# Four chunks of a graph layer's front made ahead instead of five, the fourth late chunk with a row buffer of its own

## The reference

```python
h = jnp.maximum(_layernorm(x, axis=-1), 0.0)          # x: (4096, 256)
rowsum = adj.sum(axis=1)                              # adj: (4096, 4096)
d_inv_sqrt = jnp.where(rowsum > 0, rowsum ** (-0.5), 0.0)
normalized_adj = d_inv_sqrt[:, None] * adj * d_inv_sqrt[None, :]
out = (normalized_adj @ h) @ W + b                    # W: (256, 256)
x = x + relu(out)
```

## Time and profile before

| | |
|---|---|
| median of three runs | 395.7 us (395.69 to 397.05) |
| the profiled execution | 396.11 us, its span 394.3 us |
| TensorE matmuls busy | 383.9 us, 97% of the span |
| VectorE busy | 319.9 us, 81% |
| ScalarE busy | 287.7 us, 73% |
| GpSimd busy | 117.2 us, 30% |
| read from HBM, written | 147.33 MB, 4.22 MB |

### The profile page before, as it was taken

How to read it: one execution, slowest core, us unless ns; L and a number is a source line. 1 busy time by engine, 2 the same in 40 slices (tenths; PEclk the granted TensorE clock), 3 DMA queues, 4 the chain that set the end, 5 groups by cost and what they waited for, 6 DMA issues and landing times.

```text
span 394.3 us, 5160 instructions
## 1 busy us (share of the span) xinstructions
PE 383.9 (97%) x1750; PEld 318.4 (81%) x1750; DVE 319.9 (81%) x313; ACT 287.7 (73%) x283; POOL 117.2 (30%) x278
## 2 busy tenths in 40 slices
PE   6997999999999999999999999999999999999995
PEld 5885788888888888888888888888888888878884
DVE  4948958978686999959689995868889497899997
ACT  2789989888787778678977869787886777365531
POOL 2450675352121126213224831323323223000000
PEclk9999999999999999999999999999999999999998
DMA  8999999999999999999999999999999986898457
GB/s 283 423 421 418 420 421 421 419 422 423 412 421 421 418 421 421 416 422 421 418 421 421 421 415 422 416 419 423 421 419 412 408 310 218 318 369 325 135 190 262
DMA packets 24217, 151.87 MB, mean 385 GB/s; under 512 B 3328, under 2 KB 3328, under 8 KB 7552
## 3 DMA queue, kind: packets, MB, share of 16 engines
q1 hardware_dynamic: 24192, 151.55, 95.1%
HBM read 147.33 MB, written 4.22 MB: 384 GB/s over the span
## 4 chain that ended last, share of the span: by engine, by line
PE 83%; DMA 8%; DVE 3%; ACT 3%; issue 1%; SPq 1%; POOL 1%; DVEq 0%; ACTq 0%; POOLq 0%
PE moved L840 20%; PE moved L842 19%; PE moved L841 19%; PE held L840 6%; PE held L842 6%; PE held L841 6%; DMA out<-nat 3%; DMA out<-turned 3%; PE held L791 2%; DMA acc<-in_x 1%; DMA turned<-in_x_t 1%; ACT nat L398 1%; DVE lo L652 1%; PE moved L775 1%; PE moved L809 1%; PE moved L811 1%
## 5 line engine op out<-in xcount | busy, mean ns | idle before, releaser
L411 ACT ACTIVATE hi<-at,s 128x1024 fp32r<-128x1024 f32 x112 | 123.0, 1145 | 47.3 <-issue 32.4
L840 PE MATMUL moved<-hi,G 128*128 128x512 f32 x384 | 149.9, 390 | 2.6 <-DVE lo L652 1.2
L652 DVE SCALAR_TENSOR_TENSOR lo<-at,s,hi 128x1024 fp32r<-128x1024 f32 x112 | 141.0, 1278 | 12.5 <-ACT hi L411 12.5
L841 PE MATMUL moved<-lo,G 128*128 128x512 f32 x384 | 149.5, 389 | 0.0
L842 PE MATMUL moved<-hi,G 128*128 128x512 f32 x384 | 149.4, 389 | 0.0
L671 DVE TENSOR_TENSOR acc<-moved,acc 128x1024 f32<-128x1024 f32 x84 | 102.7, 1223 | 50.3 <-PE moved L842 50.0
L398 ACT ACTIVATE nat<-nat 128x2048 f32<-128x2048 f32 x64 | 122.0, 1908 | 6.0 <-DMA nat<-in_adj 5.9
L840 PEld LDWEIGHTS moved<-hi,G 128*128 128x128 f32 x384 | 72.1, 188 | 19.1 <-issue 2.9
L842 PEld LDWEIGHTS moved<-hi,G 128*128 128x128 f32 x384 | 72.1, 188 | 15.0
L841 PEld LDWEIGHTS moved<-lo,G 128*128 128x128 f32 x384 | 72.1, 188 | 14.9
L549 POOL TENSOR_TENSOR row_sum<-part 128x1 f32<-128x1 f32 x32 | 18.0, 562 | 182.5 <-ACT nat L398 182.5
(11 more groups left out here) (69 smaller groups left out, 246.3 us busy)
## 6 DMA issues: line engine op xcount, KB each, us to landing
nat<-in_adj SPq DMA_DIRECT2D x64, 1024.0 KB, 13.2
at<-in_adj_t SPq DMA_DIRECT2D x64, 1024.0 KB, 11.9
acc<-in_x SPq DMA_DIRECT2D x4, 512.0 KB, 7.6
nat<-d_dram SPq DMA_DIRECT2D x2, 1024.0 KB, 5.9
nat<-in_x_t SPq DMA_DIRECT2D x4, 512.0 KB, 4.1
turned<-in_x_t SPq DMA_DIRECT2D x4, 512.0 KB, 4.8
out<-nat SPq DMA_DIRECT2D x4, 512.0 KB, 4.9
turned<-in_x SPq DMA_DIRECT2D x3, 512.0 KB, 14.6
```

The costliest lines, as they stand in the source:

```text
L411: nc.scalar.activation(hi[g % RING][:, 2 * c:2 * c + 2, :], at[g % LA][:, 2 * c:2 * c + 2, :], ACT.Copy, scale=s[:, j:j + 1]).then_inc(hi_ ...
L652: nc.vector.scalar_tensor_tensor(out=lo[g % RING][:, tiles, :], in0=at[g % LA][:, tiles, :], scalar=s[:, j:j + 1], in1=hi[g % RING][:, til ...
L840: nc.tensor.matmul(into[:, f, :], big, hi[g % RING][:, t, :], start=begins, stop=False)
L841: nc.tensor.matmul(into[:, f, :], big, lo[g % RING][:, t, :], start=False, stop=False)
```

## The change

AHEAD falls from 5 to 4: chunk 4 is no longer made in the front but late, and the late chunks are made in steps 4, 6, 8 and 10 and projected in steps 5, 7, 9 and 11. The rows of a late chunk get a buffer of their own, late_rows; the wait for the turned buffer moves from the load of the rows to the load of x_late. Chunk 3 is the one in the front that is projected by parts. The fourth early half row is summed on VectorE, with a semaphore of its own. x of chunk 1 is issued from ScalarE's queue. From slot 2 on nat_table is one half row less ahead. TensorE's warming transposes are 16 instead of 14, with five more behind the first turned half chunk. In slot 0 the first block of both panels comes before the second block. ScalarE and VectorE work slot 1 before they take the rounding and the rest of chunk 2's product. The diff, without unchanged code:

```diff
-AHEAD = 5
-MADE_IN = {5: 5, 6: 8, 7: 11}
+AHEAD = 4
+MADE_IN = {4: 4, 5: 6, 6: 8, 7: 10}
...
-FIRST_PART = 4
-WARM = 14
+FIRST_PART = 3
+WARM = 16
+FILL = 5
...
-        end = min(EARLY + min(2 * (g + 1), g + 4) + max(0, g - 20) // 8, 2 * NB)
+        end = min(EARLY + min(2 * (g + 1), g + 3) + max(0, g - 20) // 8, 2 * NB)
...
+        late_rows = sb("late_rows", [P, BW * D])
...
         def h(c):
-            flat = acc[:, c, :, :].rearrange("p f r -> p (f r)") if c < AHEAD else turned[c % 2][:, :]
+            flat = acc[:, c, :, :].rearrange("p f r -> p (f r)") if c < AHEAD else late_rows[:, :]
...
+        def wait_summed(eng, m):
+            eng.wait_ge(nat_summed, m + 1 if m < EARLY - 1 else m)
+            if m >= EARLY - 1:
+                eng.wait_ge(last_early_summed, 1)
...
             def load_x(c):
-                if c >= AHEAD:
-                    sp.wait_ge(hW_done, min(c - 1, AHEAD))
-                    at_least(sp, hT_parts_ready, parts_count(c - 2))
+                if c > AHEAD:
+                    sp.wait_ge(mean_ready, 2 * c)
...
             def save_mean(c):
                 sp.dma_start(means_dram[c - AHEAD], minus_mean[:, c * BW:(c + 1) * BW]).then_inc(mean_saved, DMA)
+                sp.wait_ge(hW_done, min(c - 1, AHEAD))
+                at_least(sp, hT_parts_ready, parts_count(c - 2))
                 sp.dma_start(hT(c), x_late[c - AHEAD]).then_inc(x_late_landed, DMA)
...
             def load_nat(m):
-                at_least(sp, nat_summed, m - LN + 1)
+                if m >= LN:
+                    wait_summed(sp, m - LN)
...
-            load_x(1)
             for c in range(2, AHEAD):
                 load_x(c)
                 load_nat(c - 2)
+            load_nat(EARLY - 2)
             load_nat(EARLY - 1)
...
                 if k == LAST and q == 1:
-                    sp.wait_ge(nat_summed, 2 * NB)
+                    wait_summed(sp, 2 * NB - 1)
...
+            act.dma_start(h(1), x[1]).then_inc(x_landed[1], DMA)
             take_first_half()
...
-                if c >= 2:
-                    sum_nat(c)
-            sum_nat(EARLY - 1)
+            sum_nat(EARLY - 2)
             round_slot(0)
+            round_slot(1)
             round_raw(AHEAD - 2)
-            round_slot(1)
             round_raw(AHEAD - 1)
...
             def scale_of(j):
-                pool.wait_ge(nat_summed, 2 * (j + 1))
+                wait_summed(pool, 2 * j + 1)
...
             rstd_of(0)
-            means_of(4)
             scale_of(0)
...
+            def sum_last_early():
+                m = EARLY - 1
+                dve.wait_ge(nat_landed[m % LN], DMA)
+                nc.vector.reduce_sum(part[:, m // 2, m % 2:m % 2 + 1], nat[m % LN][:, :],
+                                     axis=mybir.AxisListType.X).then_inc(last_early_summed, 1)
...
-            take_stats(1, first)
             centre(0, second)
-            take_stats(1, second)
+            take_stats(1)
             centre(1)
...
+            sum_last_early()
             rest_of_raw(AHEAD - 3)
             rest_of_turned(AHEAD - 1)
             for c in range(2):
                 subtract(0, c)
-            rest_of_raw(AHEAD - 2)
             for c in range(2):
                 subtract(1, c)
+            rest_of_raw(AHEAD - 2)
...
             turn(0, range(BW // 2))
+            for _ in range(FILL):
+                nc.tensor.transpose(moved[1][:, 0, 0:P], ident[:, :], ident[:, :])
...
-            for c, n in ((1, 2), (2, 1), (3, 0)):
-                if n:
-                    project(c, range(n))
+            for c, n in ((1, 2), (2, 1)):
+                project(c, range(n))
                 turn(c + 1)
                 project(c, range(n, BW))
-            project_parts(4)
+            project_parts(3)
             for g, (k, q, panels) in enumerate(SLOTS):
+                if g == 0:
+                    for c in range(WIDTHS[k]):
+                        for p, i in enumerate(panels):
+                            multiply(k, p, i, g, p, c)
+                    continue
```

More of the change, by code:

```diff
@@ L250, in build @@
         nat_summed = sem("nat_summed")
+        last_early_summed = sem("last_early_summed")
         s_ready = sem("s_ready")
@@ L812, in project_parts, with multiply @@
                 mm.then_inc(hW_done, 1)
-            def multiply(k, pos, i, g, p):
-                if i < HELD:
+            def multiply(k, pos, i, g, p, only=None):
+                if only is not None and only > 0:
+                    into = pair_of(("panel", k, i))
+                elif i < HELD:
                     into = held[i]
@@ L824, in multiply @@
                 outer = [(c, f) for f in range(FD) for c in range(WIDTHS[k])] if (k, pos) == (LAST, NP - 1) else \
-                    [(c, f) for c in range(WIDTHS[k]) for f in range(FD)]
+                    [(c, f) for c in range(WIDTHS[k]) for f in range(FD) if only in (None, c)]
                 for c, f in outer:
@@ L847, in multiply @@
                         project_parts(PROJECTING[k])
-                if (k, pos) != (LAST, NP - 1):
+                if (k, pos) != (LAST, NP - 1) and only in (None, WIDTHS[k] - 1):
                     mm.then_inc(panel_done, 1)
```

## The result

The changed kernel takes 400.39 us (median of 6 runs, 399.38 to 400.91), the kernel before 396.96 us on the same chip: ratio 1.0093, 95% interval 1.0077 to 1.0109, so 3.7 us slower. The forecast was slower, 398.0 us; the time lies 0.7 us above the upper end of the range. Part of that distance is the base and not the change: the forecast stands on 395.7 us, the median of three executions of the kernel before, and this comparison on 396.96, the median of six. Against 395.7 the ratio gives 399.4 us, inside the range; the loss itself, 3.7 us by the ratio, is still 1.4 us more than the 2.3 that was forecast. All ratios here compare undisturbed executions; only one was left out as slow, of e11 (556.6 us at a mean granted clock of 0.656).

The account below looks back on a forecast made before the run. TensorE's matmuls bound the kernel from slot 2, with VectorE nearly as full and last at the end. Front -2.15, projection +2.8 and tail +1.6 gave +2.3 us on the profiled execution, median 398.0 us against 395.7; range 395.4 to 399.7.

Parts of the forecast that it names:

- what bounds the kernel: Whole kernel: matmuls set the time from slot 2 on; before it, a chain of 13.0 us from s of block 1.
- the projection: Step 5: the fourth late chunk's 24 matmuls come back on a full TensorE, adding 2.8 us.
- what feeds GpSimd: Front: inputs GpSimd needs before s of block 1 come net 0.3 us later, between 0.8 sooner and 0.5 later.
- the second queue: Front: chunk 1's x from ScalarE's queue delays the first half of chunk 0; 1.1 us loss taken, bounds nothing to 1.25.
- the new order: Front: VectorE's centring of chunk 0's second half no longer waits behind chunk 1's landing and statistics; gain 0.8 us.
- Rival (3): Front: TensorE's pause before chunk 3's matmuls drops the clock to 0.50, costing up to 1.5 us: 399.5; chance 0.08.
- the front: Start to slot 2: s of block 1 at 28.3, 2.15 us sooner, so slot 2 at 41.3.
- the tail: From slot 55: G of block 31 one slot later delays x_out and slot 59; +1.6 us, bounds 0 and 2.2.
- nothing gives it back, tail +1.6: Tail: VectorE, 1.6 us late at slot 59, has no idle time behind it, so the kernel ends 1.6 later.
- (1): Tail: x_out lands in time, costing at most 0.7 us; kernel not slower, 396.3 to 397.1; chance 0.20.
- (2): Front: chunk 1 lands beside chunk 0 without harm, s of block 1 at 26.9: 396.5; chance 0.09 alone, 0.08 with (1).
- (4): Front: chain not relieved, ScalarE's third sum or slot 0 itself late; gain only 1 us, 399.1; chance 0.07.

Follow-up runs that it names:

- e11: Kernel before with the changed front edits, five chunks, rstd later, slot 2 loaded early, g + 3 and two x_out loads ahead of the wait for G: ratio 0.9942.
- e1: Kernel before with one edit, adjacency half rows one less ahead (g + 3 for g + 4): ratio 1.0057 to the kernel before.
- e2: Changed kernel with adjacency half rows as far ahead as before (g + 4): ratio 1.0058 to the kernel before.
- e4: Kernel before with the 24 matmuls of chunk 5's projection done twice in step 6: ratio 1.0076 to the kernel before.
- e9: Changed kernel with the first two x_out loads issued ahead of SP's wait for G of block 31: ratio 1.0044 to the kernel before.
- e7: Changed kernel with g + 4, x of chunk 1 from SP, and rstd of chunk 1 after s of block 1: ratio 1.0072 to the kernel before.
- e3: Changed kernel with x of chunk 1 issued from SP's queue again: ratio 1.0092 to the kernel before.
- e12: e3 with 26 transposes of the identity in TensorE's pause before chunk 3's matmuls: ratio 1.0101 to the kernel before.
- e5: Changed kernel with 24 instead of 16 warming transposes at the start: ratio 1.0097 to the kernel before.
- e8: e7 with five chunks in the front and three late ones, as in the kernel before: ratio 0.9962 to the kernel before.
- e6: Changed kernel with both g + 4 and x of chunk 1 from SP: ratio 1.0056 to the kernel before.

## Why the forecast came out as it did

**Right: what bounds the kernel.** That only the start of slot 2 counts, that from s of block 1 to slot 2 it is 13.0 us and remains so, and that GpSimd is last before s of block 1, hold in the profile (13.0 us in the changed kernel, in e1, e2, e4 and e9; e7 for GpSimd). They hold only while the adjacency of slot 2 is there: in e3 and e12 it takes 14.2 and 14.7 us from s of block 1. The forecast named no such limit.

**Right: the projection.** 2.8 us forecast, 2.79 measured, 2.78 in e4.

**Wrong in size: what feeds GpSimd.** The forecast took 1.1 us of loss for the second queue, against 0.8 of gain by the new order. The half landed 1.5 us later, beyond the bound of 1.25; the delay of that landing and the order's gain alone leave 0.4 us (e5), close to the 0.3 taken. The step that failed is the term for the second queue: it took the late landing to cost its own length and nothing more. The pause that it made in TensorE's work brought the lower clock with it, for which the forecast had nothing in this place, and that cost 1.5 us (e5 against the changed kernel). e2 and e9 have the same front. Their windows print 1.00 there, but the durations say otherwise: the five transposes behind the pause took 1.27 us in both, against 0.71 in the changed kernel, and the first four matmuls of chunk 0's projection 1.95 and 1.46 us, against 2.05 in the changed kernel and 1.10 in e5. Chunk 1's projection began at 14.80 and 14.66 us. So TensorE was slow in this stretch in all three profiles, at a cost of 1.2 to 1.5 us, whether its clock had fallen or had not yet risen. The executions that were timed don't settle how often: the mean granted clock of the changed kernel's six is 0.993 twice (400.75 and 400.91 us) and 0.997 or 0.998 four times (399.38 to 400.42 us), that of e5's six 0.990 to 0.997.

Rival (3) knew the mechanism, but put it into the pause before chunk 3's matmuls; the clock fell after the first pause, of 1.64 us, which the same edit had made. In the place where the forecast looked for it, it cost nothing (e3 and e12). By the page "TensorE: Matmul & The Clock Gate" of the Trainium skill, section "HAM oscillation — how this bites in real kernels", waits between bursts of matmuls bring the low level back. The windows at 8.1 us here and at 24.3 us in e3 agree with that; the pause of 3.40 us in e7, behind which the clock was at 1.00, does not. By the page "DMA: Bandwidth & Descriptors" of the Trainium skill, section "Issuing engines are not separate DMA queues", loads of two issuers interleave on the same 16 engines. With that the trace agrees: both loads issued at 0.72 us landed within 0.2 us of each other, at 4.9 and 5.1 us.

The feeding came 1.8 us later than before (22.61 against 20.79) instead of 0.3, and from there to s of block 1 GpSimd was 0.3 us quicker than forecast. So the front gave 0.92 us instead of 2.15, 1.2 of the 2.3 us that the profiled execution lies above the forecast.

**Wrong in size: the tail.** 1.6 us forecast, 2.6 measured. G of block 31 between the remainders, the later x_out load and VectorE's wait before slot 59 came as worked out: issued 5.5 us later against slot 55, at 354.1 + 1.9 = 356.0 forecast, 355.6 landed. (The 1.9 us is how much later slot 55 starts.) At slot 59 VectorE was 1.2 us late, not 1.6 (358.86 against 355.77 + 1.9). The step that failed is "nothing gives it back, tail +1.6": it followed the wait up to the first output and no further. Behind the same wait SP's queue holds slots 60 to 63 and then, each behind the last, the stores and the reloads of the x_out buffers. The first store took 11.5 us to land (361.55 to 373.08), against 8.5 before (358.46 to 366.94), since it runs behind those loads, of which the last landed at 371.84, against 364.27 before; the last reload landed at 393.28, after TensorE's last matmul at 391.98, where before it had landed 2.6 us ahead of it. VectorE's 1.40 us there, less the 0.4 by which slot 59 was better than forecast, are the other 1.0 us. e9 shows that 2.0 of the 2.6 us hang on what is queued behind the wait.

**Rivals.** (1), cover in the tail, is out by e1. (2), a second queue without harm, is out by the landing at 4.86. (4) named the gain that the front really had, 1 us, but for another cause: ScalarE's third sum ended at 25.3 us and slot 0 began at 27.96, and neither held s of block 1. The chance of 0.53 for slower by over 0.5% stood with the right sign; the range was too low at the top because two terms that erred in the same direction had each been given an upper end that was no end, and because the base had moved by 1.3 us.

## What to carry to other kernels

A step taken out of a front that waits on something else is no gain (in e7, with four chunks, s of block 1 came 3.1 us sooner than in e8 with five, and yet slot 2 began later, since its adjacency landed later), while the same step in a loop whose engine is full is paid in full: look first at what the front's last link waits for, and shorten that. Where a signal moves to a later slot, list everything queued behind the wait for it, down to the last store, and not only the next user. And before a chain is shortened, look at what lands next: here every microsecond won at s of block 1 beyond 1.5 ran into the landing of slot 2 until its load was moved.

## What the runs showed of the hardware

The granted clock fell to 0.50 after a pause of 1.64 us (changed kernel, before 6.67 us) and of 2.72 us (e7, before 38.85 us), and at the end of pauses of 3.03 us (e3) and 3.21 us (e6). It stayed at 1.00 through pauses of 1.20 us, before 32.14 us, and of 1.61 us, before 36.75 us, in the changed kernel itself, and through one of 3.40 us, before 24.61 us, in e7. The length of one pause alone thus doesn't decide, and these runs don't say what else does. With work that nobody reads put into the pause (e12) or ahead of it (e5) the clock was at 1.00 in the one profile of each; that the added work is the reason is likely for e5, which removes the pause, and not shown for e12. A window can print 1.00 where TensorE runs at the lower rate (e2 and e9 ahead of 9.8 us, by the durations), so the durations of like instructions are to be looked at beside it. And two loads of 256 and 512 KB issued at the same moment by two engines landed together: the smaller took 4.1 instead of 2.6 us.
